# Attention scores of two heads side by side on the half rows of TensorE, with queries and keys in two fp16 parts

## The reference

```
Q, K, V = proj(Wq, bq), proj(Wk, bk), proj(Wv, bv)
_, top_idx = jax.lax.top_k(jnp.linalg.norm(Q, axis=2), 409)
Q_sel = jnp.take_along_axis(Q, top_idx[:, :, None], axis=1)
scores = jnp.einsum('bud,bld->bul', Q_sel, K) * 16 ** -0.5
attn = jax.nn.softmax(scores, axis=-1)
out_sel = jnp.einsum('bul,bld->bud', attn, V)
out_full = jnp.zeros((32, 2048, 16)).at[jnp.arange(32)[:, None], top_idx].set(out_sel)
x = x + ga * (out_full.reshape(2, 2048, 256) @ Wo.T + bo)
```

## Time and profile before

| | |
|---|---|
| time, median of 3 runs | 1194.58 us (1193.07 to 1196.31) |
| span of the profiled execution | 1193.6 us |
| PE busy (matmuls) | 993.4 us, 83% |
| DVE busy | 904.4 us, 76% |
| POOL busy | 713.0 us, 60% |
| ACT busy | 646.3 us, 54% |

### The profile page before, as it was taken

One profiled execution on the slowest core, in us unless ns is written; L12 is line 12 of the kernel. 1 busy time (PEld: TensorE's weight loads), 2 busy tenths in 40 slices (PEclk: granted clock), 3 DMA queues, 4 the chain that ended last, 5 costly groups with the idle time before them and its releaser, 6 DMA issues. The chain is left out here.

```text
span 1193.6 us, 29414 instructions
## 1 busy us (share of the span) xinstructions
PE 993.4 (83%) x7725; PEld 611.1 (51%) x7726; DVE 904.4 (76%) x2197; ACT 646.3 (54%) x1448; POOL 713.0 (60%) x840
## 2 busy tenths in 40 slices
PE   7999101399999999999977873299999999999995
PEld 4444000233333333333324662287778888888894
DVE  4895588778888888888866887667778777777774
ACT  2777185157777777777763441355454444444441
POOL 1687482447888888888659992124445544554443
PEclk9999655569999999999997895599999999999998
DMA  6244772201111111111306991399982322322332
GB/s 229 105 143 164 234 243 79 59 19 44 39 47 34 46 34 46 34 46 34 84 21 205 259 272 41 77 235 226 218 204 50 50 43 48 53 44 44 53 45 27
DMA packets 129229, 118.70 MB, mean 99 GB/s; under 512 B 18128, under 2 KB 117136, under 8 KB 129168
## 3 DMA queue, kind: packets, MB, share of 16 engines
q1 hardware_dynamic: 106904, 95.02, 27.0%
...
...
## 5 line engine op out<-in xcount | busy, mean ns | idle before, releaser
L994 DVE TENSOR_REDUCE attend_mxh<-attend_p_a 128x1 f32<-128x512 f32 x416 | 264.1, 685 | 56.9 <-PE attend_p_a L1137 52.0
L1076 ACT ACTIVATE w<-attend_p_b 128x409 f32<-128x409 f32 x480 | 228.8, 514 | 95.1 <-PE attend_p_b L1153 89.3
L1875 ACT ACTIVATE expert_hr<-expert_p,b1t 128x256 f32<-128x256 f32 (+1 forms) x376 | 134.3, 423 | 194.1 <-PE expert_p L1813 174.1
L1768 POOL DMA_INDIRECT out_x<-expert_ys,expert_drop x72 | 121.2, 1684 | 193.6 <-DVE expert_ys L1910 138.2
L1153 PE MATMUL attend_p_b<-attend_qt,w 98*128 98x409 bf16 x480 | 164.4, 347 | 0.3 <-ACT w L1076 0.3
L1137 PE MATMUL attend_p_a<-w,attend_qt 96*128 96x512 bf16 x384 | 151.0, 397 | 1.8 <-DVE attend_mxh L994 0.9
L1835 PE MATMUL expert_p<-w,expert_hhi 128*128 x800 | 136.7, 273 | 0.5 <-DVE expert_ys L1910 0.2
L1813 PE MATMUL expert_p<-expert_xhi,w 128*128 128x256 f16 x800 | 136.3, 273 | 0.0
...
L906 POOL DMA_INDIRECT attend_qsel<-q_d,idx x96 | 92.9, 967 | 39.8 <-POOL attend_idle L934 19.4
L1163 PE MATMUL attend_p_o<-w,attend_vh 128*32 128x409 f32 x1024 | 115.2, 522 | 1.1 <-ACT w L1076 0.6
L925 POOL DMA_INDIRECT attn_d<-outs,idx x93 | 92.4, 994 | 31.8 <-POOL attend_idle L934 19.7
...
## 6 DMA issues: line engine op xcount, KB each, us to landing
expert_wu<-w SPq DMA_DIRECT2D x88, 256.0 KB
...
q_d<-project_q SPq DMA_DIRECT2D x32, 256.0 KB, 3.1
...
```

What stands on the lines that cost most here:

```text
L994: dve.tensor_reduce(mxh[:, c, k:k + 1], chunk_bank(a)[:, :], AX, ALU.max).then_inc(a_done, 1)
L1076: act.activation(prob[:, j, :], tile_bank(j)[:, 0:TOP], ACT.Exp, scale=SCALE).then_inc(prob_done, 1)
L1768: pool.indirect_dma_start(out=out, out_offset=bass.IndirectOffsetOnAxis(ap=drop[u][:, s:s + 1], axis=0), in_=ys[u][:, s, :], in_offset=Non ...
L1875: last = act.activation(hr[g % 2][:, f, rows], p_1[g][:, f, rows], ACT.Relu, bias=cst["b1t"][:, bass.ds(e[s] * FB + 2 * g + f, 1)], scale= ...
```

## The change

Queries and keys are now split into two fp16 parts each, after Q and K have been scaled (`UNIT` = 16 in the weights and the bias). A head then needs four products of parts, 64 rows with those of the maximum: the first part of Q against both parts of K, 32 rows, the second part against the first part of K, 16 rows, and two of the 16 rows between them carry the maximum in two parts. Two heads lie side by side, one in rows 0 to 63 and one in rows 64 to 127 of `kt`, `qa` and `qb`, and all is done for a pair of heads, 16 times:

- `scores_chunk` and `scores_tile` issue one matmul for each head of the pair, with `tile_position` (0, 0) and (64, 0), into two different banks. Their number in all is as before. `p_a` has four banks (shared with `turn_q`) and `p_b` three (shared with `turn_m`); `p_m` is gone.
- `values` takes four key tiles of both heads in one block, eight matmuls in the four strips of columns, so that a pair has four blocks. `results`, `products`, `turn_q` and the ACT copies come once for a pair. The four strips now hold two partial sums for each of the two heads, and `fold` is 34 columns wide.
- The queries are transposed a second time, `turn_m`, with the maximum added in the same PSUM bank, and ACT copies the whole (`queries_max`), 128 rows, in place of two rows.
- POOL's `memset`s of `idle` are gone; `turn` waits only for `a_done`.
- The pair loop is written out and not a loop of the program; the four weight pieces are split by DVE after its last maximum.
- Before the first pair DVE fills eight blocks of 32 rows of `kt` (four before), POOL gathers six chunks for the first pair, and 26 maxima are taken before the first tile.
- In the projection `third` and `third_k` and the second ACT copy are gone; the third of the four slots of a query's row in memory is zero. Keys have two parts in memory and not three.
- Seven scatters (four before) are issued in the route block's first `bias` steps.

```
-TERMS = 6
-PARTS = 3
+PARTS = 2
 HELD = 4
-STACK_K = ((0, 3), (3, 2), (5, 1))
-KR = TERMS * HD
+ROWS_H = HELD * HD
+UNIT = 16.0
+STEP_M = 256.0
...
-                    pool.tensor_tensor(heads(rest[t % R]), heads(y[t % R]), q3[t % 8][:, :, 1, :], ALU.subtract).then_inc(rest_done, 1)
-                def third(t):
-                    pool.wait_ge(part1_done, t + 1)
-                    pool.tensor_tensor(q3[t % 8][:, :, 3, :], heads(rest[t % R]), q3[t % 8][:, :, 2, :], ALU.subtract).then_inc(part2_done, 1)
+                    pool.tensor_tensor(q3[t % 8][:, :, 3, :], heads(y[t % R]), q3[t % 8][:, :, 1, :], ALU.subtract).then_inc(part1_done, 1)
...
+                    j = NB - 1
                     dve.wait_ge(k_ps, KD * NB)
-                    dve.wait_ge(krest_done, KD * (NB - 1))
-                    dve.tensor_scalar(yk[1][:, :], p_k[1][:, :], bkb[:, 1, B - 1:B], None, ALU.add).then_inc(last_y[1], 1)
-                    dve.wait_ge(k_saved[(NB - 1) % 2], 16 * KD * PARTS * ((NB - 1) // 2))
-                    dve.tensor_scalar(k3[(NB - 1) % 2][1][:, 0, :], p_k[1][:, :], bkb[:, 1, B - 1:B], None, ALU.add).then_inc(last_first[1], 1)
-                    dve.wait_ge(kpart2_done, KD * (NB - 1))
+                    dve.wait_ge(k_saved[j % 2], 16 * KD * PARTS * (j // 2))
+                    dve.tensor_scalar(k3[j % 2][1][:, 0, :], p_k[1][:, :], bkb[:, 1, B - 1:B], None, ALU.add).then_inc(last_first[1], 1)
                     for oc in range(KD):
-                        dve.wait_ge(last_y[oc], 1)
                         dve.wait_ge(last_first[oc], 1)
-                        dve.tensor_tensor(krest[oc][:, :], yk[oc][:, :], k3[(NB - 1) % 2][oc][:, 0, :], ALU.subtract).then_inc(last_rest, 1)
-                    for oc in range(KD):
-                        dve.wait_ge(last_second, oc + 1)
-                        dve.tensor_tensor(k3[(NB - 1) % 2][oc][:, 2, :], krest[oc][:, :], k3[(NB - 1) % 2][oc][:, 1, :], ALU.subtract).then_inc(last_third, 1)
+                        dve.scalar_tensor_tensor(out=k3[j % 2][oc][:, 1, :], in0=p_k[oc][:, :], scalar=bkb[:, oc, B - 1:B], in1=k3[j % 2][oc][:, 0, :],
+                                                 op0=ALU.add, op1=ALU.subtract).then_inc(last_second, 1)
...
+        NP = N // 2
+        HP, CHP, TIP = 64, 2 * NA, 2 * TPB
+        BLOCKS = TPB // 4
+        QB, KB = 3, 4
...
-        p_a = [ps(f"p_a{i}", [P, 512], F32) for i in range(3)]
+        fold = sb("fold", [P, 2 * W1], F32)
+        p_a = [ps(f"p_a{i}", [P, 512], F32) for i in range(4)]
         p_b = [ps(f"p_b{i}", [P, 512], F32) for i in range(3)]
         p_o = ps("p_o", [P, 512], F32)
-        p_m = ps("p_m", [P, 512], F32)
...
+                def turn(p, at):
+                    wait(pool, a_done, min(CHP * (p + 1) + 6 + 2 * at, CHP * NP))
...
-                    pool.memset(idle[:, 0:width], 0.0).then_inc(idled, 1)
-                    pool.wait_ge(idled, next(rows))
...
+                for p in range(KB):
+                    for h in range(2):
+                        load_rows(p, h)
+                    sp.wait_ge(fill_done, 2 * p + 2)
+                    for h in range(2):
+                        load_again(p, h)
...
+                for p in range(KB):
+                    for h in range(2):
+                        dve.memset(kt[p][HP * h + 32:HP * h + 64, :], STEP_M).then_inc(fill_done, 1)
...
+                for p in range(NP):
+                    for a in range(3, 6):
+                        maxima(p + 1, a)
+                    if p > 0:
+                        finish(p - 1)
+                    for a in range(6, NA):
+                        maxima(p + 1, a)
+                    if p + 1 < NP:
+                        minus_maximum(p + 1)
+                    for a in range(3):
+                        maxima(p + 2, a)
...
+                def queries_max(p):
+                    act.wait_ge(mq_ps, p + 1)
+                    wait(act, b_ps, TIP * (p - 1))
+                    act.activation(qb[p % 2][:, 0:TOP], p_b[max_use(p) % 3][:, 0:TOP], ACT.Copy).then_inc(mq_done, 1)
+                def probability(p, j, h):
+                    act.wait_ge(b_ps, TIP * p + 2 * j + h + 1)
+                    if h == 0:
+                        wait(act, pv_ps, BLOCKS * (p - (j < TPB // 2)) + (j % (TPB // 2) + (TPB // 2 if j < TPB // 2 else 0)) // 4 + 1)
+                    act.activation(prob[:, 2 * (j % (TPB // 2)) + h, :], p_b[tile_use(p, j, h) % 3][:, 0:TOP], ACT.Exp, scale=SCALE / UNIT ** 2).then_inc(prob_done, 1)
...
+                def turned(q, into, low):
+                    last = None
+                    for c in range(QT):
+                        cols = slice(c * P, min((c + 1) * P, TOP))
+                        for h in range(2):
+                            n = 2 * q + h
+                            tail = slice(32 * (n % GH), 32 * (n % GH) + QTAIL)
+                            for r in range(2):
+                                w = 2 * h + r
+                                source = qsel[q % QB][:, h, c, 32 * r:32 * r + 32] if c < FULL else qtail[n // GH % 2][:, 32 * r:32 * r + 32]
+                                last = pe.matmul(into[32 * w:32 * w + 32, cols], source, cst["identb"][:, :] if c < FULL else cst["identb"][:, tail],
+                                                 start=True, stop=not (low and r), tile_position=(0, 32 * w))
+                                if low and r:
+                                    k = P if c < FULL else QTAIL
+                                    last = pe.matmul(into[32 * w:32 * w + 32, cols], mpart[0:k, h, c, :], cst["identb"][0:k, 0:k],
+                                                     start=False, stop=True, tile_position=(0, 32 * w))
+                    return last
...
+                    for h in range(2):
+                        use = chunk_use(q, a, h)
+                        wait_chunk_bank(pe, use)
+                        into, rows = p_a[use % 4], slice(HP * h, HP * h + HP)
+                        if c < FULL:
+                            last = pe.matmul(into[:, :], qa[q % 2][rows, c * P:(c + 1) * P], kt[q % KB][rows, k * CH:(k + 1) * CH], start=True, stop=True, tile_position=(HP * h, 0))
+                        else:
+                            for w in range(NK):
+                                last = pe.matmul(into[32 * w:32 * w + QTAIL, :], qa[q % 2][rows, c * P:TOP], kt[q % KB][rows, w * CH:(w + 1) * CH],
+                                                 start=True, stop=True, tile_position=(HP * h, 32 * w))
...
+                    for h in range(2):
+                        use = tile_use(p, j, h)
+                        wait_tile_bank(pe, use)
+                        rows = slice(HP * h, HP * h + HP)
+                        pe.matmul(p_b[use % 3][:, 0:TOP], kt[p % KB][rows, j * P:(j + 1) * P], qb[p % 2][rows, 0:TOP],
+                                  start=True, stop=True, tile_position=(HP * h, 0)).then_inc(b_ps, 1)
...
+                    pe.wait_ge(prob_done, TIP * p + 8 * (b + 1))
+                    for i in range(4):
+                        for h in range(2):
+                            w, j = 2 * h + i % 2, 4 * b + i
+                            last = pe.matmul(p_o[32 * w:32 * w + VC, 0:TOP], vh[p % 2][:, j, h, :], prob[:, 2 * (j % (TPB // 2)) + h, :],
+                                             start=(b == 0 and i < 2), stop=(b == BLOCKS - 1 and i > 1), tile_position=(0, 32 * w))
...
+                for p in range(NP):
+                    scores_tile(p, 0)
+                    scores_tile(p, 1)
+                    scores_chunk(p + 1, 3)
+                    scores_tile(p, 2)
+                    if p > 0:
+                        values(p - 1, 3)
+                    scores_tile(p, 3)
+                    scores_chunk(p + 1, 4)
...
-                    if isinstance(t, int) and t < QT:
+                    if isinstance(t, int) and t < LAST:
                         scatter_last(t)
```

631 lines of the change are left out of this document (294 added, 337 removed).

## The result

The changed kernel took **1163.28 us** (median of 4 runs, 1161.83 to 1163.96), the kernel before beside it 1193.82 (4 runs, 1192.17 to 1196.31): a ratio of 0.974, 95% interval 0.973 to 0.976. The profiled execution took 1163.02, its span is 1161.1. Forecast were 1166 and a range of 1143 to 1206. All times are of fast runs: one of e1's four executions, 1262.9 us, was a slow one and is left out.

The account below looks back on a forecast made before the run. PE was taken as the bound before; afterwards no engine fills a pair and the order decides. -5.3 + 11.7 - 38.6 + 3.5 = -28.7 from 1193.6 gives 1164.9, with 1.0 for the median 1166 us; range 1143 to 1206.

Parts of the forecast that it names:

- projection: End of the projection: DVE begins its last-keys work later but with less of it, and two transfers replace three; -5.3 us.
- selection: The selection behind the projection: a chain on DVE that only shifts, costed at nothing.
- start of the attention: Before the first tile: eight DVE fills for four, then 26 maxima; first tile at 37.0 us instead of 25.3, +11.7.
- first tile to the last `finish`: Attention pairs: 15 at 20.8 us, 3 for the low clock, last pair 23.0; 338.0 against 376.6, -38.6.
- from there to the end: Route block: POOL is busy there, so three more scatters of 1.0 to 1.4 us each are paid; +3.5 (0 to 5).
- The pair: One pair of heads in the attention: 20.8 us, against 23.3 for two heads before.
- ACT's gaps behind the value blocks: In each pair ACT stands idle around values and `results`, together 6.3 us, on top of 14.4 of work.
- the walk: Stepping through one pair in PE's written order with prices per piece: 20.8 us a pair, 23.0 for the last.
- up to 4 more: Projection: extra gain in us if the removed copies and subtractions on ACT and POOL had held PE; costed at nothing.
- if each fill has the 0.48 ahead of it: Start of the attention: a possible 3 us more on top of the +11.7, from time ahead of each DVE fill.
- The `idle` memsets go: Attention: removing POOL's memsets gives nothing, as POOL is not the bound; gathers may bunch up but `a_done` spaces them.
- The clock rival: Attention: PE, no longer full, drops to the low clock for half of the pairs; 44 us more, 1210; chance 0.10.

Follow-up runs that it names:

- e1: The changed kernel with both heads' tiles and chunks computed on the same rows 0 to 63: 1246.1 us, ratio 1.039 to the kernel before.
- e5: The changed kernel with each maximum reading 256 of the 512 columns: 1222.8 us, ratio 1.022 to the kernel before.
- e9: The changed kernel with three of the last pair's seven scatters in the route block left out: 1220.5 us, ratio 1.019 to the kernel before.
- f0: The changed kernel run again later on chip C, nothing edited: 1219.1 us, ratio 1.019 to the kernel before.
- f3: The changed kernel with POOL's 512-column memsets put back ahead of the attention's gathers and scatters: 1186.5 us, ratio 0.992 to the kernel before.
- f5: The changed kernel with 256-column POOL memsets, also ahead of the second pair's gathers, and DVE fills of 128 partitions: 1175.9 us, ratio 0.982 to the kernel before.
- f2: The changed kernel with the turned queries moved between chunks 8 and 9 of the next pair: 1220.2 us, ratio 1.020 to the kernel before.

## Why the prediction was right, and where it holds

In the result's runs the whole was right, and so was the step that carries it; some other steps were off and partly made up for each other. The sum was -28.7 on the spans, measured -32.5 (1193.6 to 1161.1):

| step | forecast | measured |
|---|---|---|
| projection | -5.3 | -8.3 (134.62 to 126.32) |
| selection | 0 | +0.85 (87.22 to 88.07) |
| start of the attention | +11.7 | +13.4 (25.2 to 38.6) |
| first tile to the last `finish` | -38.6 | -39.1 (376.6 to 337.5) |
| change to the route block | 0 | -2.4 (3.9 to 1.5) |
| from there to the end | +3.5 | +3.1 (566.0 to 569.1) |

- **The pair**, the step that carries it: 20.8 walked, 20.73 measured; the sum of PE's work with overlapping halves and of ACT's gaps behind the value blocks stood. The gaps were forecast at 1.9, 0.8, 1.0, 1.3 and 1.3, together 6.3, and measured at 1.86, 0.76, 0.89, 1.23 and 1.01, together 5.75; ACT is busy for 14.9 of the pair, 14.4 by the sum. e1 shows the overlap by its counterpart. That DVE is not the bound is read from its 3.0 us of idle time in a pair (3.3 forecast); e5 shows it only with pauses in the pairs. That the gaps could be closed by smaller value blocks was not shown.
- **First tile to the last `finish`**: that this came within 0.5 us is luck. The 15 pairs took 309.6 us from the first tile to the last pair's (253.00 to 562.62), where the sum had 312 and 3 for the low clock; the first pair, granted 0.82 in the mean, took 20.1 and lost nothing. The last pair took 27.9, not the 23.0 of the walk. The clock fell there, which was in no step: three of the five value blocks in this stretch last 2.7 to 2.95, and the others 1.58. The busy times from the last turn of the maximum on:

```profile
561.82:590.60 28.78, 23.48 (x158) 7.34 (x150) 9.08 (x16) 15.70 (x37) 8.27 (x6) 0.82 0.07 21
```

- **Projection**: PE reached its last keys 1.6 us earlier (within the "up to 4 more"), and ACT's queue held two transfers for 2.0, not 2.7.
- **Start**: the 3 us "if each fill has the 0.48 ahead of it" came true (8 x 2.25, first maximum at 19.7 and not 17); the turn behind it was a little cheaper.
- **Block change**: the scatters left out of the attention's end let POOL issue its last one by 582, 9 us before DVE's end, where it was 622.3 against 623.7 before; that the block used to wait for this is argued, not shown. It was not in the sum.
- **Scatters**: 3.5 forecast, 2.1 to 2.5 by e9. The stretch that e9 is measured over grew by 4.5 (136.6 to 141.1), and what follows it shrank by 1.5; the rest of both is open. The clock is no cause: in the block's first 100 us it was granted at 0.86 before and at 0.85 after.

For f0's runs the forecast would have failed, with 1219 for 1166, 13 us beyond its range. The step that fails there is "The `idle` memsets go: POOL is not the bound in the attention, nothing". The danger was seen and dismissed: "without them gathers may bunch up, but `a_done` advances by a pair of maxima each 1.2 us, as far apart as a gather costs". 1.26 us apart is what they are where they come in a row; the memsets made it 1.77, and f3 shows that putting them back takes off 32.6 of the 56 us. The clock rival (1210) is a part of the rest, but not by its own reason: PE at 46.4 of 50 us kept 1.00 in the result's profile, and in the stretch of f0 shown above the clock fell behind a pause.

**What stays open.** Why the run of the result shows no pauses, with the same program and gathers 1.26 apart there too, and those on chips A to C do. Whether it is the chip or the moment was not tested. What holds up PE's small matmuls: by f0's last pair but one and f3's start it is there while POOL issues gathers or scatters in a row. It is not POOL's share of the time, since f3 has POOL busy for 42.5 of 50 us and f0 for 26.3. But f3 and f5 change both the distance of gathers and scatters and the times at which DVE and POOL work side by side, and no run parts these. f2 excludes the neighbours of the turned queries. The Trainium skill (SBUF — State Buffer, "Who interferes with whom") has only DVE and GpSimd wait for each other in SBUF, and PE for nobody; the runs show PE's results depend on what POOL issues, by whatever way, and don't show that SBUF is the place. The pauses stand at changes between half rows and column strips, and the Trainium skill (TensorEngine Tiling, Key Properties) says that a change of mode drains the array. The turn of the maximum is such a change too: its copy began 0.22 us behind its last matmul in f0 as in the result's profile, but late in some pairs of f3 and f5. So no run here shows whether such a change is needed for a pause. The kernel before has no trace from chips A to D. Its first gathers stand 1.25 apart, too; beside the result its copy of the turned queries is not late (0.69 behind them), and the 2 to 4 us that it takes more on A to D would leave room for a pause there.
